# Order of the routing operations inside a piece's step, and the place of the last four region clears

## The reference

```
def _unipool_layer(xt, router, W1, W2):          # xt: 2048 x 128
    probs = softmax(xt @ router)                 # 16 experts
    w, idx = max(probs), argmax(probs)
    for i in range(16):                          # W1[i]: 128 x 512, W2[i]: 512 x 128
        h = silu(xt @ W1[i]) @ W2[i]
        out += where(idx == i, w, 0) * h
    return out
for router in routers:                           # 4 layers, the same experts in each
    xt = _unipool_layer(xt, router, W1, W2)
x = x + xt
```

## Time and profile before

| what | value |
| --- | --- |
| median of the runs | 589.2 us, of 591.73, 589.2 and 586.32 |
| profiled execution | 582.74 us, span 581.0 us |
| mean granted TensorE clock | 0.93 of full speed |
| PE matmul busy | 492.7 us (85%) |
| DVE busy | 337.3 us (58%) |
| ACT busy | 294.8 us (51%) |
| POOL busy | 193.6 us (33%) |
| chain that ended last | PE 57%, DVE 16%, POOL 8%, issue 7%, ACT 7%, DMA 3% |

### The profile page before, as it was taken

One profiled execution on the slowest core, in us unless ns is written; L12 is line 12 of the kernel. 1 busy time (PEld: TensorE's weight loads), 2 busy tenths in 40 slices (PEclk: granted clock), 3 DMA queues, 4 the chain that ended last, 5 costly groups with the idle time before them and its releaser, 6 DMA issues.

```text
span 581.0 us, 16450 instructions
## 1 busy us (share of the span) xinstructions
PE 492.7 (85%) x5865; PEld 417.4 (72%) x5865; DVE 337.3 (58%) x912; ACT 294.8 (51%) x785; POOL 193.6 (33%) x238
## 2 busy tenths in 40 slices
PE   1689999999788879898778999787799887889992
PEld 1367777777655639897773998774699786479991
DVE  3467877787558674444436654555455445465672
ACT  1277776777571526554421665440466543166660
POOL 8342333231030035302235530233551042563385
PEclk9999999999898789998877999896899989799996
DMA  5643223300089734500001100000110000111143
GB/s 141 184 121 94 64 79 94 94 3 4 3 317 387 265 94 143 214 1 20 16 26 36 43 17 2 20 29 23 44 34 6 3 33 15 34 46 27 11 38 27
DMA packets 39052, 41.43 MB, mean 71 GB/s; under 512 B 5056, under 2 KB 26944, under 8 KB 38976
## 3 DMA queue, kind: packets, MB, share of 16 engines
q1 hardware_dynamic: 31024, 30.68, 16.1%
q0 software_dynamic: 5888, 8.63, 6.7%
q10 hardware_dynamic: 2064, 1.08, 0.7%
HBM read 16.65 MB, written 23.72 MB: 69 GB/s over the span
## 4 chain that ended last, share of the span: by engine, by line
PE 57%; DVE 16%; POOL 8%; issue 7%; ACT 7%; DMA 3%; DVEq 1%; ACTq 0%; POOLq 0%
PE bank L933 17%; PE bank L915 14%; PE bank L710 6%; PE bank L691 4%; POOL out_dram L430 4%; PE bank L669 3%; DVE pp L1300 2%; ACT pp L599 2%; DVE ppT L1045 2%; DVE yrows L1316 2%; PE bank L663 1%; DMA xin<-expert_rows,source_i 1%; PE bank L650 1%; PE bank L639 1%; PE bank L883 1%
## 5 line engine op out<-in xcount | busy, mean ns | idle before, releaser
L1300 DVE SCALAR_TENSOR_TENSOR pp<-pp,bank 128x512 f32<-128x512 f32 x124 | 85.2, 687 | 109.5 <-ACT pp L599 109.5
L933 PE MATMUL bank<-w,pp 128*128 x992 | 143.0, 290 | 4.4 <-issue 2.3
L915 PE MATMUL bank<-vm,ppT 128*128 x992 | 140.5, 286 | 0.1
L933 PEld LDWEIGHTS bank<-w,pp 128*128 128x128 f32 x992 | 127.7, 201 | 10.1 <-issue 7.4
L915 PEld LDWEIGHTS bank<-vm,ppT 128*128 128x128 f32 x992 | 125.5, 198 | 1.1 <-issue 0.6
L599 ACT ACTIVATE pp<-bank 128x512 f32<-128x512 f32 x124 | 74.2, 598 | 98.0 <-PE bank L915 98.0
L389 POOL DMA_INDIRECT expert_rows<-yrows,place_i x48 | 46.6, 972 | 150.4 <-DVE place_i L1197 140.3
L587 ACT COPY ppT<-w 128x512 f32 x124 | 76.6, 618 | 35.6 <-DVE piece_tile L1264 31.6
L492 ACT ACTIVATE pp<-bank,nmax 128x128 f32<-128x128 f32 x256 | 67.8, 424 | 0.0
L406 POOL DMA_INDIRECT xin<-expert_rows,source_i x48 | 46.2, 963 | 37.2 <-PE bank L904 25.7
L1316 DVE SCALAR_TENSOR_TENSOR yrows<-bank,wpiece,yrows 128x128 f32 x124 | 43.1, 347 | 24.4 <-PE bank L933 18.9
(11 more groups left out here) (205 smaller groups left out, 653.7 us busy)
## 6 DMA issues: line engine op xcount, KB each, us to landing
expert_rows<-zero_rows SPq DMA_DIRECT2D x16, 1056.0 KB, 11.7
w<-in_L_ffn_W_dram SPq DMA_DIRECT2D x32, 256.0 KB, 3.4
cx<-in_ctx_dram SPq DMA_DIRECT2D x16, 128.0 KB, 2.5
token_rows<-yrows ACTq DMA_DIRECT2D x1, 1056.0 KB, 6.7
out_dram<-xs SPq DMA_DIRECT2D x1, 1024.0 KB, 13.9
xs<-in_x_dram SPq DMA_DIRECT2D x1, 768.0 KB, 5.7
expert_rows<-yrows,place_i POOLq DMA_INDIRECT x48, 2.3
xin<-expert_rows,source_i POOLq DMA_INDIRECT x48, 2.6
```

Of the source, the lines that this page charges most:

```text
L915: last = mm(banks[2 + j % 2][:, c * P:(c + 1) * P], w1_piece[:, j % 2, c * P:(c + 1) * P], xT[:, ds(tile_of[j] * P, P)], start=True, stop= ...
L933: last = mm(banks[6 + j % 2][:, 0:D], hh[:, j % 2, c * P:(c + 1) * P], w2[:, ds(e * FF + c * P, P)], start=(c == 0), stop=(c == FC - 1))
L1300: v.scalar_tensor_tensor(hh[:, j % 2, :], th[:, j % 2, :], 1.0, banks[2 + j % 2][:, :], ALU.add, ALU.mult).then_inc(s["h_ready"], 1)
```

## The change

On all three engines the routing operations of a part move to the end of the step, and `put` moves one step later as well. On ACT `exponentials` is issued after the tanh and the copy of the transposed tile; before, it stood ahead of both. On PE `ranks` is issued after y(i-2) and the logits, before it stood ahead of them. On DVE `choose` and `weigh` are issued after the accumulation of y(i-2), before they stood between the gating and the accumulation. `put` runs in steps 24, 27 and 30 for parts 0 to 2, where it ran in 23, 26 and 29, at the very end of the step; that of part 3 ran in step 32 and now follows the last step. On SP the last four clears wait for the fourteenth transposed input tile of layer 0; before, they waited for the eighth.

```diff
# SP
-            sp.wait_ge(s["xT_mm"], NT // 2)
+            sp.wait_ge(s["xT_mm"], NT - 2)
             for e in range(E - 4, E):
                 clear_region(e)
# ACT, step(i)
                         a.copy(xT[:, i * P:(i + 1) * P], banks[i % 2][:, 0:P]).then_inc(s["xT_evac"], 1)
-                    if routes:
-                        for b in ending(i - 19):
-                            exponentials(layer + 1, b)
                     if 0 <= i - 1 < PIECES:
...
                     if routes and 0 <= i - 18 < NT - 1:
                         evac_yT(layer, i - 18)
+                    if routes:
+                        for b in ending(i - 19):
+                            exponentials(layer + 1, b)
# PE, step(i)
                         transpose_y(i - 18)
-                    if routes:
-                        for b in ending(i - 20):
-                            ranks(r, b)
                     if 0 <= i - 2 < PIECES:
...
                     if routes and 0 <= i - 18 < NT - 1:
                         logits_y(i - 18)
+                    if routes:
+                        for b in ending(i - 20):
+                            ranks(r, b)
# DVE, step(i)
                                                ALU.add, ALU.mult).then_inc(s["h_ready"], 1)
-                    if routes:
-                        for b in ending(i - 19):
-                            choose(r, b)
-                            weigh(r, b)
-                        for b in ending(i - 20):
-                            put(r, b)
                     if 0 <= i - 2 < PIECES:
...
                     if routes:
                         for b in ending(i - 18):
                             largest(r, b)
+                        for b in ending(i - 19):
+                            choose(r, b)
+                            weigh(r, b)
+                        for b in ending(i - 21):
+                            put(r, b)
                     elif 0 <= i - 17 < NT:
                         finish(i - 17)
 
                 piece_steps(step)
                 if routes:
+                    put(r, 3)
                     largest(r, 4)
```

## The result

| | before | after |
| --- | --- | --- |
| median of the runs, us | 587.88 (586.32 to 591.73, 4 runs) | 558.39 (556.42 to 559.44, 4 runs) |
| profiled execution, us | 582.74, span 581.0 | 559.43, span 557.7 |
| mean granted clock | 0.930 | 0.962 |

The ratio is 0.9485, 95% interval 0.9426 to 0.9545: 29.5 us faster by the medians. 551 with 542 to 569 was forecast, so the direction and the range hold, and about 8 of the 38 us are missing. The time lies just outside the prediction's own narrower range (544 to 557) and at the lower edge of rival (a)'s 558 to 575: the time alone can't tell these two apart, the profile has to.

A forecast was written before the change was run, and what follows sets the result against it. PE's transposes waiting for DVE's accumulation at routing layers' ends were taken as the bound. Gains of 14.5, 11.2 and 12.3 us sum to 38.0, other terms 0 net: 589.2 - 38 = 551 us, range 542 to 569.

The forecast's parts named there:

- rival (a): At layer ends, each of 12 parts keeps a wait of about 0.8 us plus half-clock time: 570 us; chance 0.21.
- The walk: Engine timing walked from h(21) to tile 15's transpose: 21.7 to h(30) plus 5.2, 26.9 us a layer.
- Ranks: On PE at the ends of steps: its own work stays on PE's path, 0.43 us for each part.
- Neither is held up: DVE's gating of 22, 0.53 us late, and accumulation of 21 delay neither y(22) nor tile 6's transpose; slack some 0.3 us.
- The tail: From h(30) to the transpose of tile 15: 5.2 us, with DVE's the last wait.
- The step that failed: POOL's scatters of a part start a step later, but the next gather waits for the last part's: no cost.
- The put: On DVE, at the end of steps 24, 27 and 30: 0.69 us each, hidden in a pause, costs nothing.
- The tail on POOL: After the steps, part 3's three scatters end before part 4's first is due: margin 0.5 us, cost 0.
- The clears: On SP in layer 0: the same 4.1 us loss six steps later, 0 net; bounds 4.1 either way.
- (b): One-hot rows miss PE's step, each part costs 3.8 us: slower, about 597 us; chance 0.05.
- (c): No change: the waits go but POOL's scatters hold the layer end; chance 0.03 with the like.
- The base: The 38 us, from the profiled execution of 582.74, was put to the median: 589.2 - 38 = 551 us.

The follow-up runs named there:

- second profiled execution: The kernel before, unchanged, profiled once more: 592.5 us, span 590.8, one run.

## Why the prediction was right, and where it was short

**DVE's, ACT's and PE's order: right.** The walk gave 9 x 2.27 + 3 x 0.43 = 21.7 us from h(21) to h(30), and with the scatters out of the way or spaced out the runs have 21.3 to 22.05. The transposes' wait fell from 20.6 to 1.0 us (under 8 was forecast), and the clock is full where it was 0.69. Inside the sum two terms are off and cancel. Ranks cost less than I took: without late news, steps with them take 2.48 to 2.54 for parts 0 and 1 and 2.60 to 2.68 for part 2, so 0.2 to 0.4 instead of 0.43. And "Neither is held up" was too good: the step from h(23) to h(24), behind the late accumulation of piece 21, takes 2.41, 2.45 and 2.78 instead of 2.27. In layer 2 that accumulation ends at 445.38 and the transpose of tile 6 starts at 445.43; together it is 0.8 us in three layers. The tail, walked at 5.2, is 5.13 to 5.18.

**The step that failed** is one clause: "Its scatters on POOL start a step later, but the next gather waits for the last part's", costed at nothing. I looked at when POOL had to be done, and at whether DVE work lengthened its calls (it did not: 967 to 1032 ns), and not at what the calls do to the engines beside them. The earlier trace rows could not tell. Three or four back to back beside PE at full speed held PE's completions up by as much as 2.2 us. The price is 9.5 us between h(21) and h(30), by the kernel that only spaces them, and the whole gap at the ends was 90.5 - 80.7 = 9.8. That kernel's 551.45 us is the number forecast for the change. The prediction named its own sign for this: "I am wrong if a step stays above 3 us." Steps of 3.05 to 4.57 us stand in all three layers, and h(21) to tile 15's transpose takes 29.8 to 30.5 us where 27 was forecast.

**The put: costed at 0, right.** A step sooner or later, it moves the steps by nothing; only its scatters do.

**The tail on POOL.** Margin 0.5, cost 0 with a bound of 0.5 a layer: measured 0.35, 0.36 and 0.47. The margin went for a reason that the walk had missed: in layer 1 `put` of part 3 was walked to start 5.15 after h(30), but waited 0.89 for PE's ranks and started at 6.01, so that POOL was free at 10.77 and not at 9.9 to 10.0. The rule that the prediction cites from the Trainium skill ("SBUF — State Buffer", the section on SBUF's two separate sides) is about VectorE operations that take the port pair shared with GpSimd; whether any operation of `choose` or `weigh` does, no row shows. The three moved scatters beside them started 1.27 to 1.28 apart and lasted 0.97, as before, so this trace shows no such loss.

**The clears: 0 net, right**, with 11.64 against 11.72 us, and 558.0 against 558.39 when they are put back.

**Rivals.** (a) A smaller stall in place of the old one, 558 to 575: the measured 558.4 touches this range, so the time alone doesn't rule it out. Its mechanism was another: PE never waited for one-hot rows in a step; what took the old wait's place came from a fourth engine. (b) Slower, for want of one-hot rows: not in this kernel. The nearest to it is the kernel with DVE's order put back, where DVE waits for ranks and the time is 599. (c) fell.

**The base.** 38 us was taken from a profiled execution 6.5 us under the median, and then subtracted from the median. The second profiled execution took 9.8 us more than the first, and 5.6 of them lie in the very stretches that the change shortens: by the same walk it would have given 124.3 - 80.7 = 43.6. The medians of before, too, lie between 587.2 and 591.2 from one series of runs to the next. So a gain counted too small by up to 5.6 and a cost of 9.5 left out cancel in part, and that 558.4 came out as near as it did is luck to that extent, as is that the spaced kernel met 551 to half a microsecond.

**Open.** Why PE's completions are held is not shown. They come in a burst: in layer 1 those of ranks, of h(26) and of a transpose arrive between 365.5 and 365.6, some 0.9 us after the last call has ended. That it goes when the calls no longer stand in a row is shown for the scatters; beside the gathers it is seen, and no run removed it. Calls in a row don't suffice. How many it takes, and at what moment of a call a completion must fall, is not known either: in the spaced kernel a pair of calls goes with an accumulation of y(24) 1.83 to 1.90 after its y, 0.2 to 0.6 more than with the scatters at the end, and in the kernel after three in a row beside y(30) of layer 1 held nothing. The longer ends of the second profile of before go mostly with the clock: over them it is 0.91, 0.80, 0.82 (40.26, 42.32, 41.76 us), and 0.83, 0.91, 0.88 in the first (41.42, 38.12, 39.22 us). Why the clock differs between two executions is open.

## What to carry to other kernels

When an order is changed, ask what the engines that are left alone will now run beside: the same 16 scatter calls a layer cost nothing that the first profile of before shows, and 3 us a layer in the new order. Issue indirect transfers one a step if they have the time. If an order is changed on several engines, try it on all together: ACT's and PE's moves without DVE's were worse than none here.

## What the hardware showed unexpectedly

- TensorE's results were done but their consumers started up to 2.2 us late while POOL issued three or more indirect DMAs 1.3 us apart, in some groups of calls and not in others; the profile books part of this as "remote" or "another core or an unknown queue", on a program of one core. Beside single scatter calls 1.8 to 2.8 us apart no tanh was late.
- Register loads from tables in SBUF took three times as long beside the 1 MB clears (355 GB/s). The instructions of line 223 in the kernel after, first beside the clears, then in a quiet stretch (ns min, median, max):
```profile
L223 DVEq TENSOR_LOAD <-piece_tile x5: 300/942/1004, 238.7 to 249.8; - x5
...
L223 DVEq TENSOR_LOAD <-piece_tile x11: 300/304/316, 320.1 to 339.0; - x11
```
The steps there take 2.9 us instead of 1.9. That the loads cause it fits, and was not tested by itself.
